# Row maxima of five heads made beside the expert products, those of the other 27 spread over attention with a lead of up to a head

## The reference

```
x  = x + attention(layernorm(x)) + experts(layernorm(x))     # x: 2 x 2048 x 256
x  = x + state_space(layernorm(x)) + dense(layernorm(x))

attention: 16 heads a batch, each with two score maps (a = 0, 1), head size 8, causal
    p[a] = softmax(mask(q[a] @ k[a].T))          # 2048 x 2048 for each map
    out  = (p[0] - lambda * p[1]) @ v            # then normed, scaled, projected
experts: 8 experts, the best 2 for each row, silu(x @ g) * (x @ u) @ d, plus a shared one
```

## Time and profile before

| | |
|---|---|
| time, median of 3 runs | 3400.95 us (3396.87 to 3401.06) |
| profiled execution: time / span | 3401.26 us / 3399.5 us |
| PE busy | 3188.7 us (94%) |
| DVE busy | 2788.6 us (82%) |
| ACT busy | 2316.7 us (68%) |
| POOL busy | 1601.0 us (47%) |
| mean granted TensorE clock | 0.977 of full speed |

### The profile page before, as it was taken

How to read it: one execution, slowest core, us unless ns; L and a number is a source line. 1 busy time by engine, 2 the same in 40 slices (tenths; PEclk the granted TensorE clock), 3 DMA queues, 4 the chain that set the end, 5 groups by cost and what they waited for, 6 DMA issues and landing times. The chain is left out here.

```text
span 3399.5 us, 61118 instructions
## 1 busy us (share of the span) xinstructions
PE 3188.7 (94%) x19814; PEld 1279.1 (38%) x19815; DVE 2788.6 (82%) x4945; ACT 2316.7 (68%) x3660; POOL 1601.0 (47%) x2080
## 2 busy tenths in 40 slices
PE   7997999989999999999999999769999999999987
PEld 4654666632222222222222222343334334333333
DVE  6766334689999999999999999258899989898997
ACT  4444333358887887888788788657877767777763
POOL 2113300024444434444333444207888888888885
PEclk9999999989999999999999999889999999999998
DMA  5442211111111110111111010141222222222221
GB/s 169 131 151 91 78 56 53 48 42 29 53 45 40 39 34 27 31 36 36 36 33 34 25 34 27 46 136 59 69 75 81 71 73 69 73 87 66 76 78 50
DMA packets 160889, 211.63 MB, mean 62 GB/s; under 512 B 32324, under 2 KB 108364, under 8 KB 160604
## 3 DMA queue, kind: packets, MB, share of 16 engines
q1 hardware_dynamic: 141340, 172.51, 16.6%
q0 software_dynamic: 8512, 18.76, 1.8%
q10 hardware_dynamic: 10752, 16.78, 1.5%
HBM read 154.48 MB, written 52.69 MB: 61 GB/s over the span
## 5 line engine op out<-in xcount | busy, mean ns | idle before, releaser
L1439 ACT ACTIVATE prob<-psS 128x1024 f32<-128x1024 f32 (+3 forms) x1280 | 1104.0, 906 | 280.2 <-PE psS L1623 270.8
L1489 DVE TENSOR_REDUCE pmax<-psR 128x1 f32<-128x512 f32 x1674 | 1057.2, 684 | 79.9 <-PE psR L1565 47.6
L2265 POOL TENSOR_TENSOR hc<-h_d,crep 128x512 f32<-128x512 f32 x512 | 647.7, 1273 | 186.8 <-DVE h_d L2494 136.5
L1565 PE MATMUL psR<-kslab,qslab 48*128 48x512 bf16 (+3 forms) x2480 | 653.0, 352 | 22.2 <-DVE pmax L1489 14.0
L1638 PE MATMUL psVo<-prob,vaug 128*32 128x512 f32 (+3 forms) x5120 | 630.8, 546 | 1.5 <-ACT ov L1443 0.8
L1623 PE MATMUL psS<-qslab,kslab 51*128 51x512 bf16 (+3 forms) x2560 | 533.4, 353 | 39.8 <-ACT prob L1439 22.6
L2494 DVE TENSOR_TENSOR_SCAN h_d<-a,state,psU 128x512 f32<-128x512 f32 x384 | 489.4, 1275 | 0.0
L1354 POOL TENSOR_SCALAR_AFFINE_SELECT prob<-prob 128x256 f32<-128x256 f32 (+1 forms) x512 | 214.0, 421 | 533.1 <-ACT prob L1439 533.1
L2484 DVE TENSOR_TENSOR psU<-dtx,psX 128x512 f32<-128x512 f32 x512 | 356.0, 695 | 89.6 <-PE psX L2644 38.8
L1565 PEld LDWEIGHTS psR<-kslab,qslab 48*128 48x128 bf16 x2480 | 187.3, 94 | 628.9 <-DVE pmax L1489 473.6
L2397 ACT ACTIVATE a<-dt,a_neg 128x512 f32<-128x512 f32 x512 | 366.7, 723 | 54.5 <-DVE h_d L2494 53.6
(11 more groups left out here) (351 smaller groups left out, 5045.5 us busy)
## 6 DMA issues: line engine op xcount, KB each, us to landing
crep<-c_rows_d SPq DMA_DIRECT2D x256, 256.0 KB, 3.1
x_e<-rows_d SPq DMA_DIRECT2D x72, 128.0 KB, 2.0
y_d<-y SPq DMA_DIRECT2D x72, 128.0 KB, 1.7
q_d<-parts SPq DMA_DIRECT2D x48, 128.0 KB, 2.4
k_d<-parts SPq DMA_DIRECT2D x48, 128.0 KB, 2.3
qslab<-q_d SPq DMA_DIRECT2D x60, 96.0 KB
kslab<-k_d SPq DMA_DIRECT2D x60, 96.0 KB
wg<-n_L_ffn_gate_proj_w_dram ACTq DMA_DIRECT2D x8, 512.0 KB, 4.1
```

The lines of the kernel that those rows point to most:

```text
L1439: act.activation(prob[g % BUFS][:, :, off:BLK], psS[g % 2][:, :, off:BLK], ACT.Exp).then_inc(prob_ready, 1)
L1489: dve.tensor_reduce(into[:, lo:lo + (count - 1) * NEXT + 1:NEXT], psR[at % BANKS][:, 0:count * w].rearrange("p (n w) -> p n w", w=w), AX.X ...
L1565: ins = pe.matmul(dst[:, m * w:(m + 1) * w], qslab[u][rows, i * P:(i + 1) * P], kslab[u][rows, ch * BLK:ch * BLK + w], start=(m == 0), sto ...
L2265: pool.tensor_tensor(hc[:, g % CR], h[:, g % HR], crep[:, g // PAIR % SPR], ALU.mult).then_inc(hc_ready, 1)
```

## The change

The maxima of heads 0, 1, 5, 13 and 21 (350 items) are made beside expert tiles 6 to 71, about 5.3 a tile in four places of a tile instead of three, and the results (`nmax_early`) are kept until their turn. The loop over tiles is written out on each engine. Two sets of `qz`, and keys in slabs 0 to 3 and one more (`kmore`), let GpSimd load the next head's while one is worked on. In attention 27 heads' items are left. `max_schedule` gives each step 0.88 times as many as before, without a gap, so that a head's items may lie up to a head earlier, and its turn with them; the turns come 7 to 58 steps ahead of the head's first score (before: 6). Slabs are loaded three heads ahead. The 14 items at the start of attention are gone; the first items in the steps are those of head 2.

```diff
+EARLY_HEADS = (0, 1, 5, 13, 21)
+
+def max_schedule(steps_of_head):
+    pace = (1, 2, 3, 0, 1, 2, 2, 1, 1, 3, 2, 3, 1, 2, 2, 1, 1, 4, 1, 2, 3, 0, 2, 2, 0, 3, 1, 3, 0, 3, 2, 1, 2, 1, 2, 3, 1, 2, 2, 2)
+    count, rate, lead, turn, ahead = len(max_items()), 0.88, 18, 2, 3
+    late = [n for n in range(NH) if n not in EARLY_HEADS]
+    fills = [[] for _ in range(NH * steps_of_head)]
+    turn_at, due, head, x = {0: -1}, 0.0, 0, 0
+    for g in range(len(fills)):
+        due += rate * pace[g % steps_of_head]
+        while due >= 1 and head < len(late):
+            n = late[head]
+            if g < steps_of_head * (n - ahead) + lead:
+                due = min(due, float(ahead))
+                break
+            fills[g].append(("max", n, x))
+            due, x = due - 1, x + 1
+            if x == count:
+                turn_at[n], head, x = g + turn, head + 1, 0
+    for n in EARLY_HEADS:
+        if n:
+            turn_at[n] = max(turn_at[n - 1] + 8, steps_of_head * (n - ahead) + lead)
...
 def phase_experts(nc, io, keep, dram):
-        EACH = 3
-        FIRST = RT - (len(ITEMS) + EACH - 1) // EACH
-        FIRST -= FIRST % 2
+        NITEM = len(ITEMS)
+        ALL = NITEM * len(EARLY_HEADS)
+        FIRST = 6
+        PLACES = 4
...
         def items_at(i, slot):
-            x = (i - FIRST) * EACH + slot if isinstance(i, int) else -1
-            return [x] if 0 <= x < len(ITEMS) else []
+            lo, hi = (min(max(i + x - FIRST, 0) * ALL // (RT - FIRST), ALL) for x in range(2))
+            share = [lo + (hi - lo) * x // PLACES for x in range(PLACES + 1)]
+            return range(share[slot], share[slot + 1])
...
         def _(pool):
-            for a in range(2):
-                c.after(pool.memset(qz[a][:], 0.0))
+            for u in range(2):
+                for a in range(2):
+                    c.after(pool.memset(qz[u][a][:], 0.0))
...
+            pool.wait_ge(early_in, loads_done(0))
+            load_queries(1)
+            for j in range(2, len(EARLY_HEADS)):
+                pool.wait_ge(early_in, loads_done(j - 1))
+                load_keys(j)
+                pool.wait_ge(max_full, NITEM * (j - 1) + CREDIT)
+                load_queries(j)
...
         def _(dve):
             def step(i, s):
-                take_max(i, 0)
 ...
-                take_max(i, 1)
+                for slot in range(PLACES - 1):
+                    take_max(i, slot)
 ...
-                take_max(i, 2)
+                take_max(i, PLACES - 1)
...
         def _(pe):
             def step(i, s):
 ...
+                max_product(i, 0)
 ...
-                            max_product(i, 0)
+                            max_product(i, 1)
+                            max_product(i, 2)
 ...
-                max_product(i, 1)
 ...
-                max_product(i, 2)
+                max_product(i, PLACES - 1)
...
 def phase_attention(nc, io, keep, dram):
-        START += [("max", 1, x) for k in range(NSTEP) for x in EARLY[k]]
+        FILLS, TURN_AT = max_schedule(NSTEP)
...
         def _(sp):
-            for n in range(2, NH):
+            for n in range(SLABS, RING):
                 load(n)
-                maxima(n - 1)
-                if n > 2:
-                    mix_store(n - 3)
-                mix_load(n)
-                load_weights(n - 2)
+            for g in range(TOTAL):
+                n, k = g // NSTEP, g % NSTEP
+                if k == 0 and RING <= n + RING - 1 < NH:
+                    load(n + RING - 1)
+                for kind, m, x in FILLS[g]:
+                    if kind == "turn":
+                        maxima(m)
+                if k == MIX_STORE_AT and n + 2 < NH:
+                    if n:
+                        mix_store(n - 1)
+                    mix_load(n + 2)
+                    load_weights(n)
```

More of the change, by code:

```diff
@@ L733, in max_items @@
     return [(a, (full if plain else masked)[n], not plain) for at, plain, n in order for a in range(2)]
+EARLY_HEADS = (0, 1, 5, 13, 21)
+def max_schedule(steps_of_head):
+    pace = (1, 2, 3, 0, 1, 2, 2, 1, 1, 3, 2, 3, 1, 2, 2, 1, 1, 4, 1, 2, 3, 0, 2, 2, 0, 3, 1, 3, 0, 3, 2, 1, 2, 1, 2, 3, 1, 2, 2, 2)
+    count, rate, lead, turn, ahead = len(max_items()), 0.88, 18, 2, 3
+    assert len(pace) == steps_of_head and sum(pace) == count
+    late = [n for n in range(NH) if n not in EARLY_HEADS]
[15 more added lines that the diff above has]
+            turn_at[n] = max(turn_at[n - 1] + 8, steps_of_head * (n - ahead) + lead)
+    for n in range(1, NH):
+        assert turn_at[n - 1] < turn_at[n] <= steps_of_head * (n - 1) + 34
+        fills[turn_at[n]].append(("turn", n, 0))
+    return fills, turn_at
 def phase_experts(nc, io, keep, dram):
@@ L750, in phase_experts @@
         FACTOR = 3
+        MADE = 2 * RING + 8
         kslabs, qslabs = keep["kslabs"], keep["qslabs"]
@@ L798, in items_at @@
         def items_at(i, slot):
-            x = (i - FIRST) * EACH + slot if isinstance(i, int) else -1
-            return [x] if 0 <= x < len(ITEMS) else []
+            lo, hi = (min(max(i + x - FIRST, 0) * ALL // (RT - FIRST), ALL) for x in range(2))
+            share = [lo + (hi - lo) * x // PLACES for x in range(PLACES + 1)]
+            return range(share[slot], share[slot + 1])
         def steps(eng, step, first, last):
[L805 to L811, removed]
+            for i in range(first, last + 1):
                 step(i, i % 2)
@@ L1246, in phase_attention @@
         FOLDS = [fold for g in range(END) for fold in folds_at(g)]
-        FILLS = [fills_at(g) for g in range(END)]
         PLACE = {fill: at for at, fill in enumerate(START + [x for fills in FILLS for x in fills])}
@@ L1422, in _ @@
                     mix(n, k - MIX_AT)
-                if n + 1 < NH and k == K_TURN:
-                    cut_max(n + 1)
+                for kind, m, x in FILLS[g]:
+                    if kind == "turn":
+                        cut_max(m)
                 if g < TOTAL and 0 <= g - SUM_AT and (g - SUM_AT) % NSTEP == 0:
@@ L1553, in take, with slab_there @@
                 return psR[at % BANKS]
+            def slab_there(n):
+                u = n % RING
+                if n < SLABS:
+                    pe.wait_ge(keep["early_in"], 384 + 96)
+                else:
+                    pe.wait_ge(slab_in[u], 192 * (n // RING + (u >= SLABS)) + CREDIT)
             def max_products(n, x):
@@ L1585, in turn_max @@
             def turn_max(n):
-                pe.wait_ge(nmax_ready, n + 1 + CREDIT)
                 dst = take(("turn", n, 0))
-                pe.transpose(dst[0:2 * ST_T, 0:P], nmax[:], keep["ident"][:]).then_inc(ring_full, 1)
+                if n in EARLY_HEADS:
+                    rows = keep["nmax_early"][:, EARLY_HEADS.index(n)]
+                else:
+                    pe.wait_ge(nmax_ready, LATE_HEADS.index(n) + 2 + CREDIT)
+                    rows = nmax[:]
+                pe.transpose(dst[0:2 * ST_T, 0:P], rows, keep["ident"][:]).then_inc(ring_full, 1)
             def scores_free(g):
```

128 lines of the change are left out of this document (63 added, 65 removed).

## The result

The change made the kernel slower: 3431.72 us (median of 4 runs, 3426.98 to 3434.34) against 3401.01 (3396.87 to 3403.68) on the same chip, a ratio of 1.009 (95% interval 1.0072 to 1.0107). That is less than 2%, but clear of no change. Forecast were 3382 us and a range up to 3430. One execution of one kernel further down, at 5734.92 us with a lower granted clock, is left out of that kernel's time.

What follows compares the result with a forecast made beforehand. The prediction took VectorE as nearly full in attention and TensorE as full in the experts. Experts +84, start of attention +9 and heads -112 summed to -19 us, from 3401.3 to 3382 us, range 3343 to 3430.

Steps and rivals of the forecast that it cites:

- Experts: Expert phase: 280 more items 69 us, bank waits 11 and a late start 4, together 84 us longer.
- The six-item tile's 0.55 us of waiting: Expert tiles with six items: TensorE waits 0.55 us for a bank VectorE holds, 11 us in 20 tiles.
- Writing the loop out costs nothing: Experts: tiles of the loop and those outside it already run without gaps, so writing it out adds 0 us.
- The item's 0.247: Experts: TensorE time per item, from tiles of 4.70 and 5.43 us; 280 more items make 69 us.
- Tile 6: Experts: extra clears of `qz` delay its transfers, so TensorE waits at the first item, 4 us once.
- Start of attention: Head 2's first item waits for slab 2, about 7 us, plus 2 us for a longer low clock: 9 us once.
- Attention: Heads in attention: 42.0 us each, 3.6 us less a head, 112 us saved over 31 heads.
- for each quarter I take the larger: Attention heads: quarters of 10.4, 11.0, 9.6 and 11.2 us sum to 42.2 before corrections for row wait and unevenness.
- the forecast's own sign of being wrong: Prediction wrong if a middle head stays above 43 us or an expert tile averages more than 6.4 us.
- The check by the last head: Attention: the last head, without maxima, takes 40.4 us, so no schedule brings a head far below 40.
- From this comes off the wait for the turned rows, about 1 us: Attention heads: turns 7 steps ahead or more remove the wait for row transfers, about 1 us a head.
- C: Rival: TensorE's queue bounds attention, a head saves only 2.1 us, total 3429 us, slower; chance 0.20.

Runs made afterwards that it cites:

- four items: Changed kernel with all but four of the 70 items of heads 4 to 31 left out of attention, all turns kept: 3287.37 us.
- The lead alone: Changed kernel with only heads 0 and 1 beside the experts, the rest at rate 1.0, turns 38 steps or more ahead: 3422.28 us, ratio 1.0052.

## Why the prediction was wrong

**Experts: right but for its base.** +73.0 measured, 84 forecast. The six-item tile's 0.55 us of waiting came as laid out; the tiles themselves are shorter than forecast, 5.7 for 6.0 and 6.4 for 6.5 or more. "Writing the loop out costs nothing" missed a gain of 0.14 us in 44 tiles. The item's 0.247 was read from two kinds of tile, the loop's 4.70 and those with items outside it. With 4.56 as base an item is 0.216 us for its 512 columns, 0.23 with the masks, and the rest was a wait for banks that before had too. Tile 6 cost 9.5 us with the half clock behind its wait, not 4. So the sum missed by 11 us, with errors in both directions.

**Start of attention: right in size, in part by luck.** 8.3 against 9, though the wait itself was 12.2 us and not 7. Without it head 0 still takes 49.25 us, so the stall cost 7.2.

**Attention: the failing step.** It is "for each quarter I take the larger of the last head's time and the middle head's less 12% of VectorE's busy time there", with the 3.6 us a head that followed; 1.94 came, and a head above 43 us was the forecast's own sign of being wrong. Over heads 1 to 30, the quarters of a head (ten steps each, from exponential to exponential) are these:

| quarter | before | after | forecast | four items |
|---|---|---|---|---|
| 1 | 10.61 | 10.36 | 10.4 | 9.82 |
| 2 | 11.57 | 11.59 | 11.0 | 10.23 |
| 3 | 10.95 | 10.83 | 9.6 | 9.79 |
| 4 | 12.76 | 11.18 | 11.2 | 9.65 |

The first and the fourth came as forecast. The second was to lose 0.6 and the third 1.3 us, and together they lost 0.1. Of the 1.94 us, 1.58 came out of the fourth, where the turn and the wait for its rows had stood. One middle head of after by quarters (columns as in the earlier trace rows):

```profile
1368.82:1378.93 10.11, 9.71 (x80) 2.97 (x76) 8.80 (x22) 9.18 (x13) 2.91 (x7) 1.00 0.28 79
1378.93:1390.06 11.13, 10.66 (x82) 2.80 (x81) 10.07 (x21) 9.56 (x14) 7.96 (x14) 1.00 0.09 25
1390.06:1401.30 11.24, 10.98 (x91) 3.40 (x91) 9.48 (x20) 9.19 (x14) 5.10 (x10) 1.00 0.01 1
1401.30:1413.00 11.70, 11.34 (x96) 3.82 (x94) 10.26 (x17) 8.71 (x12) 3.00 (x8) 1.00 0.14 36
sum 44.18, PE 42.69 PEld 12.99 DVE 38.62 ACT 36.64 POOL 18.97; mean PE 10.67 PEld 3.25 DVE 9.65 ACT 9.16 POOL 4.74
```

The third quarter stands at 11.24 here where 9.6 was forecast, with VectorE idle for 1.76 us of it, though VectorE's 38.0 us of work a head came as forecast. The rule had two faults. It took VectorE's busy share for a bound, and the halving of its work, on both kernels, shows that it is worth 0.8 to 1.1 us a head in all. And it let a saving in one step pay in another, while 22 steps of 40 have nothing to give. The check by the last head put the floor at 40.4, a little high: part of that head ran at the half clock, and in seven of the runs here the same head takes 38.42 at the full clock. The way from there to 46 is convex, and a floor says nothing of it.

**The turn.** "From this comes off the wait for the turned rows, about 1 us": in the kernel before, TensorE's idle time on those rows was 16.7 us in all, 0.54 a head:

```profile
L1623 PE MATMUL psS<-qslab,kslab 51*128 51x512 bf16 (+3 forms) x2560 | 533.4, 353 | 39.8 <-ACT prob L1439 22.6 <-DMA qslab<-mpart 16.7
```

The wait went, but for head 0 and the last head. The turn, 7 to 56 steps ahead, costs 0.6 us a head where it now stands; its old step (34) takes 0.69 less without it. The forecast took off 0.2 for the two together (1 less 0.8). The lead alone, in its one form that was run, added 0.2.

**The rivals.** C gave 3429 with a head 2.1 us shorter, and the run 3431.7 with 1.94. Its head was nearly right. That its total was so close is partly luck: its experts were 11 us too long, and 6 us of the measured difference stand in later phases. Its price, that an item is worth in attention what TensorE needs for it, matches the last 8.6 items of a head (0.23 us), if the new placement is counted in. As a general cause it falls: halving TensorE's work on the items gave 1.4 us, not 5.9, and the next 28 items are worth 0.10 each. So no single engine sets a head. The best account of these runs is a sum over steps, in which TensorE's fixed order, VectorE's banks and ScalarE's exponentials take turns; that is argued from the step times, not shown step by step. Why the last items cost just TensorE's columns, and how much of the 0.23 is theirs and how much the turn's, is not shown by a run. The Trainium skill ("TensorEngine Tiling (Array Packing)", Theoretical Speedup) gives products of at most 64 rows up to twice the speed. The trace bears this out for the two products themselves, 0.39 us for both; among products of full height the pair gained nothing.

**The trade.** An item costs 0.23 us in the experts before any stall and, with the placement, gives back 0.23 in attention. With the stalls 280 items cost 73 us. The 258 of them that came out of heads 1 to 30 gave back 58, the 14 from the start of attention nothing (17.2 us from the last transposes of h to the first exponential before, 17.3 after), and head 0 became 8 longer. With the stalls taken out the kernel is still 0.3% slower than before (1.0013 to 1.0042). No version run here beat it.

## What to carry to other kernels

A high busy share is not a bound. Before work is moved off an engine, halve its work where it stands. Here two runs would have warned: a head lost 1.1 us with VectorE at half and 1.4 with TensorE at half, and this change, which took 12% of the items from both, had to gain 3.0 to pay. Filler work that several engines share can have a convex price, as here: the first items cost 0.06 us each and the last 0.10 to 0.23. So a move is worth only the marginal price at both ends. When a loop has steps with a hard floor, count the steps that have something to give, and don't average a saving over them.

## What the runs showed of the hardware

Two products of 48 rows in different halves of the array start together and take one's 0.39 us, but a change between products of 128 and of 48 rows costs about 0.10 us each way (0.32 from the pair's start to the next product, where 0.22 is the pitch). A stall of TensorE of 6.0 us was followed by 5.6 us at a clock of 1.2 GHz, so the tile with it took 9.5 us more than its neighbours. Expert tiles without items took 4.64 to 4.78 us inside a loop over a register and 4.56 written out.
